# A selective state space whose sums, inputs and row spreads move to TensorE and ScalarE: one kernel on one core

## The reference, cut to what matters

```
xz = x @ W_in;  xb, z = split(xz)                      # 2 x 256 channels
xb = silu(causal_conv4(xb) + conv_b)
dt_low, Bm, Cm = split(xb @ W_x, [64, 80])             # 64, 16 and 16 columns
dt = softplus(dt_low @ W_dt + b_dt)
h[t] = h[t-1] * exp(A * dt[t]) + (xb * dt)[t] * B[t]   # 256 channels x 16 states
y[t] = sum over n of h[t, :, n] * C[t, n]
out = (y + xb * D) * silu(z)
x1 = layernorm(x + out @ W_out)
```

## Time and profile before

| What | Value |
|---|---|
| time of the kernel before, median of 3 runs | 1614.55 us (1614.25 to 1616.75) |
| span of the profiled execution, first to last instruction | 1611.6 us |
| profiled span against the median | 2.95 us less |
| busy share of PE, DVE, ACT, POOL over the span | 89%, 79%, 68%, 78% |
| the state space stage | about 36 to 914 us |

### The profile page before, as it was taken

The page is one execution under the profiler, slowest core; times in us unless marked ns, Lnnn a source line. Parts: engine busy times, 40 slices in busy tenths (PEclk is TensorE's granted clock), DMA queues, the critical chain, the costliest instruction groups (busy, mean ns, idle before and its releaser), DMA issues. The chain is left out here.

```text
span 1611.6 us, 22055 instructions
## 1 busy us (share of the span) xinstructions
PE 1430.3 (89%) x6146; PEld 876.3 (54%) x6146; DVE 1269.8 (79%) x2207; ACT 1088.3 (68%) x2118; POOL 1250.6 (78%) x861
## 2 busy tenths in 40 slices
PE   4889999899989989998998799999999999539994
PEld 1334343334333433343343388888888877429993
DVE  1999999999999999999999367777777787624542
ACT  4778877887788778877886477666666655114552
POOL 1899999999999999999999444477777766624665
PEclk8999999999999999999999889999999999659997
DMA  5455465546554655465545263314418000036771
GB/s 167 154 178 182 153 198 168 184 153 205 168 184 153 196 176 176 161 197 176 169 161 159 63 220 130 136 35 142 149 47 327 14 8 13 22 112 189 210 208 38
DMA packets 126058, 236.92 MB, mean 147 GB/s; under 512 B 13490, under 2 KB 76917, under 8 KB 125952
## 3 DMA queue, kind: packets, MB, share of 16 engines
q1 hardware_dynamic: 121408, 227.21, 43.6%
q0 software_dynamic: 4544, 8.47, 1.5%
HBM read 180.89 MB, written 55.66 MB: 147 GB/s over the span
## 5 line engine op out<-in xcount | busy, mean ns | idle before, releaser
L388 POOL TENSOR_TENSOR hc<-state,c_rows 128x1024 f32<-128x1024 f32 x256 | 598.5, 2359 | 46.4 <-DVE state L585 40.7
L585 DVE TENSOR_TENSOR_SCAN state<-ps_da,inp 128x512 f32<-128x512 f32 x512 | 593.4, 1206 | 27.3 <-ACT ps_da L481 27.3
L704 PE MATMUL ps_y<-hc,ident 128*128 128x512 f32 x1024 | 491.0, 619 | 56.2 <-POOL hc L388 56.2
L481 ACT ACTIVATE ps_da<-dt,a_neg 128x512 f32<-128x512 f32 x512 | 345.4, 688 | 86.8 <-DVE state L585 84.2
L704 PEld LDWEIGHTS ps_y<-hc,ident 128*128 128x128 f32 x1024 | 194.2, 196 | 296.4 <-issue 208.6
L574 DVE TENSOR_TENSOR inp<-dtx,ps_b 128x1024 f32<-128x1024 f32 x192 | 230.8, 1202 | 37.6 <-POOL dtx L359 22.6
L1069 POOL TENSOR_TENSOR rs<-ms,m_half 128x4 f32<-128x4 f32 x48 | 67.9, 1415 | 124.0 <-DVE ms L1267 123.8
L1192 ACT ACTIVATE ex<-sc,nmx,ctx_r 77x128 f32<-77x128 f32 x192 | 92.4, 482 | 97.3 <-DVE nmx L1280 97.3
L371 POOL TENSOR_TENSOR inp<-dtx,b_rows 128x1024 f32<-128x1024 f32 x64 | 151.0, 2359 | 0.1
L627 PE MATMUL ps_misc<-x1T,w_conv 128*128 128x512 f32 (+3 forms) x256 | 118.2, 606 | 23.1 <-ACT x1T L414 23.1
L487 ACT COPY ps_b<-b_rows 128x512 f32<-128x512 f32 x192 | 111.1, 579 | 37.8 <-DVE inp L574 36.3
(11 more groups left out here) (234 smaller groups left out, 2689.6 us busy)
## 6 DMA issues: line engine op xcount, KB each, us to landing
b_rows<-bc_rows SPq DMA_DIRECT2D x128, 512.0 KB, 4.7
c_rows<-bc_rows SPq DMA_DIRECT2D x128, 512.0 KB, 4.0
sorted_x<-pad_rows SPq DMA_DIRECT2D x8, 4160.0 KB
w<-in_L_ffn_W SPq DMA_DIRECT2D x78, 256.0 KB
vw<-vw_rows SPq DMA_DIRECT2D x16, 462.0 KB
vw_rows<-vw_out SPq DMA_DIRECT2D x16, 384.0 KB
xrow<-sorted_x SPq DMA_DIRECT2D x39, 130.0 KB
x_tok<-in_x SPq DMA_DIRECT2D x16, 256.0 KB, 4.1
```

The source lines that it names most:

```text
L388: pool.tensor_tensor(hc[:, n % RING], state[:, n % RING], over_c(c_rows[:, slot, n % 2]), ALU.mult).then_inc(hc_ready, 1)
L481: act.activation(ps_da[u % DA_RING][:], dt[:, par, c], ACT.Exp, scale=a_neg[:, c, n:n + 1]).then_inc(da_ready, 1)
L585: dve.tensor_tensor_scan(state[:, n % RING, c], ps_da[u % DA_RING][:], inp[:, n % RING, c], 0.0, ALU.mult, ALU.add).then_inc(state_ready, 1)
L704: ins = pe.matmul(ps_y[:, c], ident[:], hc[:, n % RING, c], start=False, stop=n == NS - 1)
```

## The change

Five things change in the state space stage; the other two stages are the same.

1. **y is token-major.** hc is no longer a moving operand against the identity (two 128x512 products a state, L704) but is transposed into y: eight 128x128 transposes a state that accumulate in PSUM. They stand two states behind instead of one. The product with D becomes eight 128x128 products, z becomes token-major (two banks of two 128x256 products), and the gated y is transposed back and copied to SBUF by ACT ("y0", "y1") before the projection.
2. **The inputs of five states (3, 6, 7, 11, 14)** are made token-major by ACT (`scaled`: four 128x256 multiplications by a per-partition scalar) and transposed by PE into the bank that held the decay (`side_input`); the decay of such a state goes to SBUF.
3. **B rows** of the eight states that DVE feeds are spread by PE (`spread_b`, four transposes of a broadcast column) instead of copied by ACT. POOL feeds 1, 9 and 12.
4. **One silu cluster.** silu of xb and of z both stand at n = 4 on ACT, between one pair of table loads.
5. xb gets two buffers, and ACT copies the transposed B columns ("BT") and dt xb ("t0", "t1") for item 2.

```diff
-    POOL_FEEDS = [3, 7, 11, 15]
+    SIDE = [3, 6, 7, 11, 14]
+    POOL_FEEDS = [1, 9, 12]
+    DECAYS.update({2: [3, 6], 4: [5, 7], 5: [], 6: []})
+    SCALED = {0: 3, 1: 6, 3: 7, 7: 11, 12: 14}
...
-    PE_SLOT = {0: ["xT"], 1: ["xb0"], 2: ["xb1"], 5: ["dbl"], 7: ["dt0", "dt1"]}
+    PE_SLOT = {0: ["xb0"], 1: ["xb1"], 5: ["dbl"], 6: ["BT"], 7: ["dt0", "dt1"], 13: ["t0"], 14: ["t1"]}
...
+        def scaled(g, par, n):
+            at = side_at(g, n)
+            act.wait_ge(act_pre, apre("t1", g))
+            need(act, side_full, (at - 1) * C)
+            for b in range(GB):
+                ins = act.activation(inpT[:, at % 2, b], dtxT[:, b].rearrange("p c d -> p (c d)"), ACT.Copy, scale=b_tok[:, par, b, n:n + 1])
+            ins.then_inc(side_scaled, 1)
...
+                if n == 4:
+                    act.preload_act_table_set("silu_and_others")
+                    if not last:
+                        prepare(g + 1, 1 - par, "xb0")
+                        prepare(g + 1, 1 - par, "xb1")
+                    gates(g)
+                    act.preload_act_table_set("natural_log_exp_and_others")
...
+        def fill_z(g, k, last):
+            if not last:
+                pe.wait_ge(act_pre, apre(f"xb{k}", g + 1))
...
         def add_y(g, par, n):
+            pe.wait_ge(hc_ready, after(NS, n, g))
+            for b in range(GB):
+                for c in range(C):
+                    ins = pe.matmul(ps_y[:, b, c], hc[:, n % RING, c, b * P:(b + 1) * P], ident[:], start=False, stop=n == NS - 1,
+                                    is_transpose=True, skip_group_check=True)
+            ins.then_inc(y_added, 1)
...
+        def side_input(g, n, c):
+            at = side_at(g, n)
+            pe.wait_ge(side_scaled, at + 1)
+            pe.wait_ge(state_ready, op_free(g, n, c))
+            for b in range(GB):
+                ins = pe.transpose(op_bank(g, n, c)[:, b * P:(b + 1) * P], inpT[:, at % 2, b, c * P:(c + 1) * P], ident[:])
+            ins.then_inc(side_full, 1)
...
         def group(g, par, first, last):
             for n in range(NS):
+                if n + 1 in SIDE:
+                    side_input(g, n + 1, 0)
+                if n + 2 in DVE_FEEDS:
+                    spread_b(g, par, n + 2)
+                elif n + 2 == NS and not last:
+                    spread_b(g + 1, 1 - par, 0)
+                if n + 1 in SIDE:
+                    side_input(g, n + 1, 1)
+                if n == 4:
+                    fill_z(g, 0, last)
+                    fill_z(g, 1, last)
+                if n < 2 and not first:
+                    add_y(g - 1, 1 - par, NS - 2 + n)
+                if n == 4:
+                    start_y(g, par)
+                    add_y(g, par, 0)
+                    add_y(g, par, 1)
+                if n == 5:
+                    add_y(g, par, 2)
+                if n >= 5:
+                    add_y(g, par, n - 2)
+                if not first and n in (5, 6):
+                    turn_y(g - 1, n - 5, last)
```

More of the change, by code:

```diff
@@ L395, in group @@
                     feed(g + 1, 1 - par, n + RING - NS)
[L396 removed]
+        over_groups(group)
     @blk.scalar
@@ L596, in group @@
                 scan(g, par, n, 1)
-                if not first and n == 2:
+                if not first and n == 3:
                     gated(g - 1)
-                if not first and n == 15:
+                if not first and n == 12:
                     normed(g - 1)
-        over_groups(dve, group)
+        over_groups(group)
         gated(NG - 1)
@@ L650, in project @@
-        def project(g, last):
-            pe.wait_ge(yz_ready, g + 1)
-            if not last:
+                    pe.wait_ge(act_pre, apre("dbl", g))
+                    need(pe, z_gated, after(2, 0, g - 1))
+                    need(pe, yt_read, after(C, 1, g - 2))
+                else:
+                    pe.wait_ge(act_pre, apre("BT", g))
+                ins = pe.matmul(bank[:], w_dt[:, c * P:(c + 1) * P], xdbl[0:R], start=True, stop=True)
+            if name in ("t0", "t1"):
+                c = int(name[1])
+                if c == 0:
+                    pe.wait_ge(pool_pre, ppre("dtx", g))
+                    need(pe, u_read, unit("P", g - 1))
+                    need(pe, x1_ready, g - 1)
+                else:
+                    pe.wait_ge(act_pre, apre("t0", g))
+                for b in range(GB):
+                    ins = pe.transpose(bank[:, b * P:(b + 1) * P], dtx[:, par, c, b * P:(b + 1) * P], ident[:])
@@ new lines, in fill_misc @@
+            ins.then_inc(misc_full, 1)
+        def fill_z(g, k, last):
+            if not last:
+                pe.wait_ge(act_pre, apre(f"xb{k}", g + 1))
+            elif k == 0:
+                pe.wait_ge(u_read, unit("V2", g - 1))
+            else:
+                pe.wait_ge(act_pre, apre("t1", g))
+            for b in range(2):
+                at = (g * GB + 2 * k + b) * P
+                ins = pe.matmul(ps_misc[BANK[f"z{k}"]][:, b * C * P:(b + 1) * C * P], x1T[:, at:at + P], w_in[:, C * P:], start=True, stop=True)
+            ins.then_inc(z_full, 1)
@@ new lines, in turn_y @@
+        def turn_y(g, c, last):
+            if c == 0:
+                pe.wait_ge(yz_ready, g + 1)
+                if g < NG - 1:
+                    pe.wait_ge(z_gated, after(2, 0, g + 1))
+                else:
+                    pe.wait_ge(u_read, unit("V2", g))
+            else:
+                pe.wait_ge(yt_read, after(C, 0, g))
+            for b in range(GB):
+                ins = pe.transpose(ps_misc[BANK[f"y{c}"]][:, b * P:(b + 1) * P], yz[:, b, c], ident[:])
+            ins.then_inc(yt_full, 1)
@@ L730, in group @@
                 if not first and n == 9:
[L731 to L735 removed]
+                    project(g - 1)
+                if not first and n == 10:
                     variance(g - 1)
```

383 lines of the change are left out of this document (202 added, 181 removed).

## The result

| What | Before | After |
|---|---|---|
| median (runs) | 1614.8 us (1614.3 to 1616.8) | 1846.1 us (1845.7 to 1849.5; 4) |
| ratio | 1 | 1.1435 (95% 1.1419 to 1.1451) |
| profiled span | 1611.6 us | 1844.4 us |
| end of the last x1T of the stage | 914.2 us | 1149.4 us |
| granted clock from 36 us to there | 0.96 | 0.88 |

The change costs 231 us, 70 more than forecast and inside the range. All of it lies in the state space stage: its end is 235 us later, and the two stages behind it together are 2.4 us shorter. The starts of the sixteen projections split the loss: the first comes at 151.69 us instead of 126.36 (+25.3), the thirteen gaps that follow are 69.51 us on average instead of 53.97 (+202), and from the fourteenth to the last it is 84.3 instead of 79.0 (+5.3).

A forecast was written before the change was run, and what follows sets the result against it. DVE bounds now, POOL just behind; after the change a closed loop through PE's in-order stream: 28.2 + 14.1 + 20.9 = 63.2 us a group, plus 2.2 for the clock, 65.4. Forecast 1776 us (+161), range 1655 to 1890.

The forecast's parts named there:

- places 1 and 2: VectorE standing for PE: 5.5 us at feed 4 behind the convolution, 6.7 us at scan 6 behind z, D and additions.
- place 3: Before scan 8: ScalarE stands for z, y0, dbl, y1 and BT, writing the decay of 8 at 18.6 us, just in time.
- B: Stretch from the first scan of state 4 to the end of state 8's scans: 20.9 us, plus 2.2 for the clock.
- C: Stretch from the end of state 8's scans to the end of hc 15, bound by POOL's twelve operations: 28.2 us.
- A: Stretch from the end of hc 15 to the next group's first scan of state 4: 14.1 us.
- P15: The end of state 15's hc on POOL, where stretch C ends and A begins; forecast at 106 us in group 0.
- rival 1: PE's clock stays low through transposes: 7 us a group more, 1880 us, outer bound 2120; chance 0.20.
- theory A: Chain through silu, z, D, additions, y0, dbl to spread 8 and its decay is all: about 1715 us for e2.
- Theory A2: Second way round: hc 4 waits for state 0's addition behind z and D, so e2 takes 1825 to 1846 us.
- rival 2: One of the two stands is absent: 57.7 to 60 us a group, 1655 to 1685 us; chance 0.14.
- rival 3: POOL bounds, PE being ahead of DVE's needs in B and A: 49.1 us plus about 1 a group, 1535; chance 0.11.
- Rivals 2 to 4: The second and third have their own lines; the fourth: work only shifts, time the same within 0.2% (3 us), chance 0.03.

The follow-up runs named there:

- e8: The changed kernel without side inputs: POOL feeds states 1, 5, 9 and 12, VectorE the other twelve; 1752.8 us, ratio 1.0854.
- e9: e6 with variance units and x1T copy later, state 14's multiplications two states earlier, B's spread for 10 ahead of dt0 and dt1: 1610.7 us, ratio 0.9969.
- e2: The changed kernel with side inputs 6 and 7 and spread 8 ahead of z on PE, and state 8's decay earlier on ScalarE: 1794.6 us, ratio 1.1125.
- e3: As e2, with the product with D and the additions 0 and 1 also ahead of z on PE: 1784.3 us, ratio 1.1064.
- e6: The changed kernel with D, additions 0 to 2, side inputs 6, 7 and spread 8 ahead of z, state 8's decay earlier, convolution one state later: 1628.6 us, ratio 1.0082.

## Why the prediction was right, and where its size was off

The mechanism and the sign were right, and so were places 1 and 2; place 3 has no experiment of its own. The group was 65.4 us by forecast and 69.85 in the group read above (t is the end of the first scan of 4). That group is one of the long ones: every third gap is 70.7 us, the others are 68.75.

| Term | Forecast | This group | Mean of 12 groups | What made the difference |
|---|---|---|---|---|
| B, with the restart of the clock | 23.1 | 22.7 | 23.0 | scan 6 at t + 11.8 (12.3), feed 8 at t + 16.9 (17.5) |
| C | 28.2 | 29.9 | 29.2 | feed 15 waits 2.2 for PE |
| A | 14.1 | 17.2 | 17.2 | feed 4 at P15 + 10.45 instead of + 7.35 |

**The term that was mis-sized is A.** "PE adds 14 at P15 - 2.3, then half a convolution until P15 + 2.0" took x1T as ready. It was copied at 597.09 only, behind a decay and the four multiplications of state 3 on ScalarE's stream, so the convolution began 1.6 us behind P15 and not 1.4 ahead of it. The sign-post for this place, a stand of 5.5 us at feed 4, was met with 5.0 by luck: PE was 3.1 us later than forecast, and VectorE 3.6, since its scan 2 ended at P15 + 5.4 and not + 1.8. The prediction had charged ScalarE's new work to its sum (47.3 us, off the path) and not to its place in the stream. That is its own lesson on PE, not applied to ScalarE. e8 shows it from the other side: without these multiplications the convolution began 1.0 us ahead of P15, and A was 14.0 (13.1 and 14.8 in turn). C was off by less, and mostly in one group of three. There too PE stood for a copy, of vw_out, behind another such block, and in this group then ran at half clock:

```profile
580.18 1.69 ACT L528 ACTIVATE inpT<-dtxT,b_tok 128x256 f32<-128x256 f32 x4
...
582.29 1.65 PE L772 MATMUL ps_misc<-vw_w,ctxT 128*128 128x384 f32 x2 [2.76 <-ACT vw_out L508]
```

**Prices.** A multiplication took 494 ns and four in a row 1.69 us (1.71 forecast), an accumulating transpose 0.11 us (8 in 0.87), so the 66 us that the range held for slower ones were not used. POOL's plain sum held: 637.9 us over the thirteen gaps from 151.69 to 1055.32 is 49.1 a gap, as forecast. VectorE had 47.2 (46.6), ScalarE 45.0 (47.3). PE's sum was wrong in the adding: 50.8 less 27.5, plus 14.1, 4.4, 3.5 and 2.2, is 47.6 and not 44, and e9, at a clock of 0.99, measures 47.2. ScalarE's net by its own terms runs from -0.4 to +3.6. Neither enters the forecast; only rival 1's outer bound used the 44.

**A way that the prediction did not name.** In stretch B it follows VectorE. POOL's hc 4 waited 11.4 us for the addition of state 0, the first of the two in B. From hc 4 POOL has five operations of 2.33 us (hc 4, 5, feed 9, hc 6, hc 7) until it can start hc 8, which opens stretch C. In the changed kernel POOL stood only 0.64 us for VectorE within them, so this way was 0.64 us shorter than the one that the prediction summed. That the sum for B came out right is in part luck: a little less standing of VectorE, and the other way would have held, as it did in e2. There theory A alone (about 1715) was wrong by 80 us for that reason. Theory A2 had the way right, and missed what stretch A gave.

**The gap before.** The prediction called 55.2 us the present group. It was the longer one of a repeating pattern whose mean is 53.97. The forecast was counted from the starting point of the stage and not as a difference of groups, so it took no harm, but "8.0 more than now" should have been 9.2, rival 2 counted 2.5 to 4.7 us a group that were 3.7 to 5.9, and rival 3 counted 5.1 that were 3.9.

**The rivals.** Rival 1, that the clock stays low through transposes, is refuted by windows of the changed kernel (columns as in the earlier trace rows):

```profile
582.00:583.80 1.80, 1.51 (x3) 0.80 (x4) 1.46 (x2) 1.47 (x3) 1.62 (x3) 0.50 0.49 171
583.80:587.00 3.20, 3.20 (x17) 3.20 (x16) 1.32 (x2) 1.07 (x2) 3.20 (x2) 0.50 0.02 5
587.00:588.00 1.00, 1.00 (x7) 1.00 (x6) 1.00 (x2) 0.00 (x0) 1.00 (x2) 0.50 0.00 0
588.00:588.70 0.70, 0.70 (x5) 0.56 (x4) 0.70 (x2) 0.64 (x1) 0.70 (x1) 0.71 0.41 47
588.70:589.60 0.90, 0.90 (x4) 0.27 (x4) 0.44 (x1) 0.64 (x2) 0.90 (x1) 1.00 0.83 187
589.60:597.60 8.00, 4.68 (x40) 4.23 (x40) 7.35 (x7) 5.60 (x12) 6.35 (x4) 1.00 0.37 113
```

From 583.8 to 588.7 PE ran nothing but transposes, without a gap, and towards their end, at about 588.4, the granted clock rose from 0.50 (1.2 GHz) to 1.00 (2.4 GHz); from 589.6 to 597.6 it ran nothing but transposes, with 3.3 us idle, and the clock stayed up. Here a product stood ahead of the transposes. In e3, in the lines shown above, none did: behind 6.17 us idle PE ran transposes alone from 577.33, at a granted clock of 0.50 until 580.8, and from 580.9 it was 1.00, ahead of the first product at 581.09. The Trainium skill, page "TensorE: Matmul & The Clock Gate", section "Part 4: PE-mode transpose", has it that the full clock does not engage for transposes; this trace disagrees, and the measurement decides. What cost time was the standing: behind 8.94 us idle, z took 3.59 us for its eight products. In e6, where PE had stood 0.15 us, they take 1.89:

```profile
501.26 0.63 PE L804 MATMUL ps_op<-ident,inpT 128*128 128x128 f32 x4 [0.15 <-DVE state L644]
501.72 0.60 PE L796 MATMUL ps_b<-ident,b_tok 128*128 128x128 f32 x4
502.16 1.89 PE L724 MATMUL ps_misc<-w_in,x1T 128*128 128x256 f32 x8
```

That is 1.7 of the 2.2 us forecast. D, right behind, was at full pace (1.95), where the forecast had let the low clock last longer. The dip at 582 to 588, behind the 2.76 us for vw_out, was not forecast. It comes in every third group, the one with the long gap; in the group before, the same 2.76 us were not followed by one (granted clock 1.00 from 515.2 to 520.0), and the same two products took 0.91 us instead of 1.65:

```profile
515.24 0.91 PE L772 MATMUL ps_misc<-vw_w,ctxT 128*128 128x384 f32 x2 [2.76 <-ACT vw_out L508]
```

Rivals 2 to 4 did not come. Rival 3's condition, PE ahead of VectorE in both stretches, is what e6 to e9 came near to (in e9 VectorE's feeds still wait 41.1 us for PE): the loss went, but instead of the group of 50.1 us that it named, 53.6 was reached.

**Sign-posts.** VectorE's wait for PE was 306 us (forecast 230): scan 6 8.4 (7), feed 8 2.8 (3), feed 4 5.0 (5.5), and two that were not forecast, feed 13 with 1.7 and feed 15 with 2.2. ScalarE's yzT and xdbl copies waited 8.9 us a group (8). The gap is 69.5 (65).

**Where the 70 us lie.** P15 of the first group came at 111.7 us (forecast 106), the fourteen groups behind it took 69.3 each (65.4), and from there to the last x1T it was 67.6 (53). That is 5.7, 54.5 and 14.9 us, together 75 in the stage; 2.4 of the other 5 are what the two later stages are shorter. In the last group POOL's nine operations from hc 8 on took 27.0 us instead of 21, and what follows 16.7 instead of 12; the final projection ran at half clock (3.78 us against 1.88 in the earlier trace rows).

## What to carry to other kernels

When an in-order engine takes over work that others wait for, its stream needs a new order before its sums mean anything: first what depends on finished work, then what the bounding engine waits for, and last the instruction that itself waits on a slow chain (here z, behind a silu). Write down every loop through that engine, the buffer ring's among them: moving what VectorE needs ahead gave 52 us, opening the ring's way as well gave 130, and taking away only the first wait gave 9. And ask of each added block not only how long it is but which copy stands behind it.

## What the runs showed of the hardware that was not expected

- Transposes hold the full clock (589.6 to 597.6 us, plain and accumulating ones), and plain ones alone bring it back (e3, 577.33 to 580.9).
- An fp32 transpose of 128x128 costs 0.11 us at full clock and 0.21 at half (583.73 to 584.58 for four plain ones, 586.29 to 588.00 for eight that add to a sum), whether it starts a sum or adds to one.
- 8.94 us of standing were followed by the lower level, and 2.76 us were in one group and not in the next, with the same instructions around them. In e6 the clock over 300 us is 0.99, against 0.89 in the changed kernel, with no change in what PE computes.
